# The lead-in of a four-layer transformer tower: one pass over all tokens against one pass per group of tokens

## The reference

```python
h = layer_norm(emb_word[input_ids] + emb_pos[:S][None], emb_ln_s, emb_ln_b)
for l in range(4):
    q = heads(h @ Wq[l] + bq[l]); k = heads(h @ Wk[l] + bk[l]); v = heads(h @ Wv[l] + bv[l])
    a = band_attention(q, k, v, mask)            # each token sees 64 tokens to each side
    h = layer_norm(h + a @ Wo[l] + bo[l], ln1_s[l], ln1_b[l])
    h = layer_norm(h + gelu(h @ W1[l] + b1[l]) @ W2[l] + b2[l], ln2_s[l], ln2_b[l])
```

## Time and profile before

| | |
|---|---|
| time, median of 3 runs | 1876.82 us (1876.59 to 1877.55) |
| span of the profiled execution (first to last instruction) | 1874.5 us, that is 2.3 us less than the median |
| PE busy | 1483.1 us (79% of the span) |
| DVE busy | 1247.8 us (67%) |
| ACT busy | 977.2 us (52%) |
| POOL busy | 808.0 us (43%) |
| mean granted TensorE clock | 0.895 of full speed |

### The profile page before, as it was taken

How to read it: one execution, slowest core, us unless ns; L and a number is a source line. 1 busy time by engine, 2 the same in 40 slices (tenths; PEclk the granted TensorE clock), 3 DMA queues, 4 the chain that set the end, 5 groups by cost and what they waited for, 6 DMA issues and landing times.

```text
span 1874.5 us, 42615 instructions
## 1 busy us (share of the span) xinstructions
PE 1483.1 (79%) x13098; PEld 1235.0 (66%) x13098; DVE 1247.8 (67%) x3542; ACT 977.2 (52%) x2392; POOL 808.0 (43%) x1177
## 2 busy tenths in 40 slices
PE   0589889798897997998988759759668887499992
PEld 0367678677676776776767648449646766389992
DVE  4788966788767888668896652433379896434344
ACT  0378733688434885348873223225348882155550
POOL 6577333684235762247733310124356521144440
PEclk9899989899899997999998968669869996599996
DMA  4666101743005550035610000147534511257765
GB/s 105 176 149 127 36 1 33 170 86 84 1 5 138 108 121 2 1 70 140 128 33 1 1 14 1 45 138 224 173 89 100 112 22 45 97 175 237 225 212 179
DMA packets 144317, 178.26 MB, mean 95 GB/s; under 512 B 22096, under 2 KB 106128, under 8 KB 143952
## 3 DMA queue, kind: packets, MB, share of 16 engines
q1 hardware_dynamic: 136784, 158.18, 32.9%
q0 software_dynamic: 7296, 17.18, 2.8%
HBM read 132.96 MB, written 42.34 MB: 94 GB/s over the span
## 4 chain that ended last, share of the span: by engine, by line
PE 31%; DVE 14%; issue 4%; DMA 2%; ACT 2%; POOL 2%; SPq 0%; DVEq 0%; POOLq 0%; ACTq 0%
PE bank L1473 7%; DVE ptl L799 4%; PE bank L1459 2%; DVE neg_max L792 2%; PE bank L645 1%; DVE xn L912 1%; PE bank L563 1%; PE bank L1460 1%; PE bank L1463 1%; PE bank L1461 1%; PE bank L1462 1%; PE bank L1217 1%; DMA xn<-y_rows 1%; PE bank L431 1%; PE bank L584 1%
## 5 line engine op out<-in xcount | busy, mean ns | idle before, releaser
L685 ACT ACTIVATE prob<-bank,neg_max 128x192 f32<-128x192 f32 (+1 forms) x960 | 406.9, 437 | 109.3 <-DVE neg_max L792 97.0
L792 DVE TENSOR_REDUCE neg_max<-bank 128x2 f32<-128x384 f32 (+1 forms) x480 | 274.3, 572 | 99.0 <-PE bank L544 91.4
L799 DVE TENSOR_TENSOR ptl<-bank,pth 128x384 f16<-128x384 f32 (+1 forms) x480 | 275.5, 574 | 4.6 <-ACT pth L698 4.0
L563 PE MATMUL bank<-ident,prob 128*128 128x128 f32 x1536 | 268.4, 288 | 0.0
L698 ACT ACTIVATE pth<-bank 128x384 f16<-128x384 f32 (+1 forms) x480 | 244.3, 509 | 9.3 <-PE bank L563 9.2
L652 ACT ACTIVATE xx<-bank 128x256 fp32r<-128x256 f32 x256 | 95.5, 386 | 196.0 <-PE bank L431 192.0
L544 PE MATMUL bank<-kx,qx 96*128 96x192 bf16 (+1 forms) x960 | 168.1, 257 | 1.1 <-DVE xx L766 1.1
L563 PEld LDWEIGHTS bank<-ident,prob 128*128 128x128 f32 x1536 | 162.9, 143 | 0.1
L584 PE MATMUL bank<-v,pth 128*128 128x33 bf16 x1152 | 138.4, 180 | 21.2 <-DVE ptl L799 18.0
L645 PE MATMUL bank<-w,fbuf 128*128 128x192 f32 x768 | 140.7, 327 | 2.0 <-DVE h L889 2.0
L734 ACT ACTIVATE fbuf<-bank,b 128x512 f32<-128x512 f32 x96 | 65.8, 687 | 146.5 <-PE bank L453 146.4
(11 more groups left out here) (295 smaller groups left out, 4522.5 us busy)
## 6 DMA issues: line engine op xcount, KB each, us to landing
xn<-in_e_seg SPq DMA_DIRECT2D x34, 768.0 KB
w<-in_e_w SPq DMA_DIRECT2D x23, 576.0 KB
qk_rows<-fbuf SPq DMA_DIRECT2D x128, 96.0 KB, 2.3
qx<-qk_rows SPq DMA_DIRECT2D x35, 288.0 KB, 4.0
kx<-qk_rows SPq DMA_DIRECT2D x35, 288.0 KB, 5.8
qk_rows<-w SPq DMA_DIRECT2D x80, 96.0 KB, 2.3
qx<-qk_rows SPq DMA_DIRECT2D x35, 192.0 KB, 4.6
kx<-qk_rows SPq DMA_DIRECT2D x35, 192.0 KB, 5.2
```

What stands on the lines that cost most here:

```text
L563: last = nc.tensor.transpose(bank[BT[p % 2]][:, c * P:c * P + P], probs_at(p, banded, c * P, P), ident[:, :])
L685: nc.scalar.activation(probs_at(p, banded, qt * n, n), scores_at(p, n)[:, qt, :], ACT.Exp, bias=neg_max[:, b % 2, hd, qt:qt + 1], scale=1. ...
L792: nc.vector.tensor_reduce(neg_max[:, b % 2, hd, :], scores_at(p, D if banded else S), AX.X, ALU.max, negate=True).then_inc(max_ready.sem, 1)
L799: nc.vector.tensor_tensor(ptl[:, p % 2, 0:n], bank[BT[p % 2]][:, 0:n], pth[:, p % 3, 0:n], ALU.subtract)\
```

## The change

- **Position rows.** They are loaded into `places`, a part of `prob` that the attention does not yet use, and after the token numbers instead of ahead of them.
- **Gathers.** Each group has a semaphore of its own. POOL issues 8 gathers, then does the `rstd` of group 0 (for which it waits), then issues the other 8.
- **Weights.** ACT makes the two high parts as its first work, DVE the scaled bias and the two low parts. POOL has no part in it.
- **Norms by group.** DVE adds the position rows of group 0 in one instruction, does its statistics, builds the first half of `mask` while POOL makes `rstd`, does scale and shift, and builds the second half of `mask`. Then it goes through `OPENING`, with the sums and statistics of group 1 after the first 4 tiles, those of group 2 and scale and shift of group 1 after v, and those of group 3 and scale and shift of group 2 at the end.
- **POOL.** The `rstd` of groups 2 and 3 and the `hb` sums of groups 1 and 2 come after `pool_v`.
- **Table fills.** The 8 DMAs that fill `y_rows`, with the wait for `mask_ok`, are issued after the last layer's SP work.

```diff
@@ sync
-            sp.dma_start(hb[:, 0:2, :], a["L0_tok_emb_pos"]).then_inc(const_in.sem, 16)
             sp.dma_start(tok[:, :], a["x"]).then_inc(tok_in.sem, 16)
+            sp.dma_start(places, a["L0_tok_emb_pos"]).then_inc(const_in.sem, 16)
...
             load_x(0)
             sp.dma_start(row_bo[:, :], a["bo"][0, :, :].to_broadcast([P, D])).then_inc(rows_bo.sem, 16)
-            sp.wait_ge(mask_ok.sem, 1)
-            filler = flat(mask[:, :, :], "p t d -> p (t d)").bitcast(F32).rearrange("p (t d) -> p t d", d=D)
-            for s in range(2):
-                for i in range(4):
-                    sp.dma_start(y_rows[s][8 * P * i:8 * P * (i + 1), :].rearrange("(t p) d -> p t d", p=P), filler)\
-                        .then_inc(filled.sem, 16)
...
             sp_layer(L - 1)
             sp.wait_ge(wa_ready.sem, wa_ready.at(L, 1))
+            sp.wait_ge(mask_ok.sem, 1)
+            (the same 8 DMAs)
 
             sp.wait_ge(h_ready.sem, h_ready.at(L, 0))
@@ gpsimd
-                    .then_inc(gathered.sem, 16)
-            pool.wait_ge(rows_x.sem, 48)
-            pool.wait_ge(const_in.sem, 16 * 8)
-            ch.mark(nc.gpsimd.tensor_tensor(bqk[:, :], bqk[:, :], q_scale[:, :].to_broadcast([P, 3]), ALU.mult))
-            pool_weights(ch, wa, QKV).then_inc(wa_ready.sem, 1)
+                    .then_inc(gathered[t // GT].sem, 16)
+                if t == 2 * GT - 1:
+                    pool_rstd(pool, ch, 0, 1 - NG, 0, 1e-12)
+            pool_rstd(pool, ch, 0, 2 - NG, 1, 1e-12)
+            pool_ones(ch)
             pool.wait_ge(rows_bo.sem, 16)
-            for g in range(NG + 1):
-                if g < NG:
-                    pool_rstd(pool, ch, 0, g + 1 - NG, g, 1e-12)
...
+            first_sums(0)
...
             pool_v(pool, ch, 0, 0)
+            pool_rstd(pool, ch, 0, 3 - NG, 2, 1e-12)
+            for g in range(NG):
+                pool.wait_ge(gathered[g].sem, 16 * GT)
             pool_middle(pool, ch, 0, 0)
             pool_middle(pool, ch, 0, 1)
+            pool_rstd(pool, ch, 0, 4 - NG, 3, 1e-12)
+            first_sums(1)
+            first_sums(2)
@@ scalar
+            act.wait_ge(rows_x.sem, 48)
+            nc.scalar.activation(wa[0][:, 0:QKV], raw[:, 0, 0:QKV], ACT.Copy)
+            nc.scalar.activation(wa[2][:, 0:QKV], raw[:, 1, 0:QKV], ACT.Copy).then_inc(first_high.sem, 1)
             for kind, i in OPENING:
@@ vector
-            dve.wait_ge(gathered.sem, 16 * NT)
-            for t in range(NT):
-                ch.mark(nc.vector.tensor_tensor(h[:, t, 0:D], h[:, t, 0:D], hb[:, t % 2, :], ALU.add))
...
+            dve.wait_ge(rows_x.sem, 48)
+            dve.wait_ge(first_high.sem, 1)
+            (bqk, wa[1] and wa[3]: three tensor_tensor)
+            dve.sem_inc(wa_ready.sem, 1)
...
+            def first_norm(g):
+                tg = slice(GT * g, GT * g + GT)
+                rows = h[:, tg, 0:D].rearrange("p (b t) d -> p b t d", t=2)
+                dve.wait_ge(gathered[g].sem, 16 * GT)
+                ch.link(nc.vector.tensor_tensor(rows, rows, places.unsqueeze(1).to_broadcast([P, 2, 2, D]), ALU.add))
+                dve_stats(dve, ch, 0, 0, g, None)
...
+            first_norm(0)
+            first_mask(range(2 * GT))
+            first_affine(0)
+            first_mask(range(2 * GT, NT))
+            ch.done(ch.n)
+            dve.sem_inc(mask_ok.sem, 1)
+            first_open(OPENING[0:GT])
+            first_norm(1)
+            first_open(OPENING[GT:2 * GT + 3])
+            first_norm(2)
+            first_affine(1)
+            first_open(OPENING[2 * GT + 3:])
+            first_norm(3)
+            first_affine(2)
```

More of the change, by code:

```diff
@@ L209, in build_tower @@
                   for x in (probs[:, PROBS * 2 * D:PROBS * 2 * D + HEADS * VC], sb("middle", [P, HEADS * VC])[:, :])]
+        places = probs[:, 0:2 * D].rearrange("p (t d) -> p t d", t=2)
         prob_16 = flat(prob[:, :, :, :], "p a s n -> p (a s n)").bitcast(BF16)
@@ L257, in build_tower @@
         tok_in = sig("tok_in", base=0)
-        gathered = sig("gathered", base=0)
+        gathered = [sig(f"gathered_{g}", base=0) for g in range(NG)]
+        first_high = sig("first_weights_high", base=0)
         tok_ok = sig("tok_ok", base=0)
@@ L1682, in _ @@
             sp.wait_ge(wa_ready.sem, wa_ready.at(L, 1))
+            sp.wait_ge(mask_ok.sem, 1)
+            filler = flat(mask[:, :, :], "p t d -> p (t d)").bitcast(F32).rearrange("p (t d) -> p t d", d=D)
+            for s in range(2):
+                for i in range(4):
+                    sp.dma_start(y_rows[s][8 * P * i:8 * P * (i + 1), :].rearrange("(t p) d -> p t d", p=P), filler)\
+                        .then_inc(filled.sem, 16)
             sp.wait_ge(h_ready.sem, h_ready.at(L, 0))
@@ L1942, in _ @@
-            ch.done(ch.n)
[L1943 to L1948, removed]
-                        dve.sem_inc(h_ready.sem, (12, 4)[g - 1])
-                    dve_affine(dve, ch, 0, g - NG, g - 1, 1)
+            dve.wait_ge(rows_x.sem, 48)
+            dve.wait_ge(first_high.sem, 1)
+            ch.mark(nc.vector.tensor_tensor(bqk[:, :], bqk[:, :], q_scale[:, :].to_broadcast([P, 3]), ALU.mult))
@@ new lines, in _, with first_mask @@
+            ch.mark(nc.vector.tensor_tensor(wa[1][:, 0:QKV], raw[:, 0, 0:QKV], wa[0][:, 0:QKV].bitcast(F32), ALU.subtract))
+            ch.mark(nc.vector.tensor_tensor(wa[3][0:D2, 0:QKV], raw[0:D2, 1, 0:QKV], wa[2][0:D2, 0:QKV].bitcast(F32),
+                                            ALU.subtract))
+            ch.done(ch.n)
+            dve.sem_inc(wa_ready.sem, 1)
+            def first_mask(tiles):
+                for t in tiles:
+                    qt = t % 2
+                    ch.mark(nc.vector.tensor_tensor(mask[:, t, :], hb[:, 4 + qt, :],
+                                                    km[:, t // 2, qt * WIN:qt * WIN + D], ALU.min))
@@ new lines, in first_norm, with first_affine @@
+            def first_norm(g):
[4 more added lines that the diff above has]
+                dve_stats(dve, ch, 0, 0, g, None)
+            def first_affine(g):
+                if g < 2:
+                    dve.sem_inc(h_ready.sem, (12, 4)[g])
+                dve_affine(dve, ch, 0, g + 1 - NG, g, 1)
@@ L1957, in dve_layer, with first_open @@
                          if opening else None)
-            for kind, i in OPENING:
-                dve_open(dve, ch, 0, kind, i, True, first_split(0))
+            def first_open(items):
+                for kind, i in items:
+                    dve_open(dve, ch, 0, kind, i, True, first_split(0))
+            first_norm(0)
[12 more added lines that the diff above has]
+            first_affine(2)
             with dve.Fori(0, L - 1) as it:
```

11 lines of the change are left out of this document (4 added, 7 removed).

## The result

| | before | changed |
|---|---|---|
| median | 1876.59 us (5 runs, 1870.13 to 1877.55) | 1856.33 us (5 runs, 1850.11 to 1864.33) |
| span of the profiled execution | 1874.5 us | 1854.6 us |
| mean granted TensorE clock | 0.895 | 0.892 |

The ratio is 0.9912, with a 95% interval of 0.9889 to 0.9936. That is 12 to 21 us less; the forecast was 1856.6. The changed kernel's five runs lie 14 us apart, and their clocks (0.885 in the slowest, 0.895 in the fastest) go with their times. So single medians say little about an effect of a few us here.

A forecast was written before the change was run, and what follows sets the result against it. DVE was taken to set the pace, idle 17.43 us in the lead-in for the sixteenth gather. First maximum 19.0 earlier plus 1.2 gave 20.2: 1874.5 - 20.2 = 1854.3, with 2.3 around it 1856.6 us; range 1851 to 1863.

The forecast's parts named there:

- Steps 1 to 4: Lead-in: token numbers, weights, norm and rstd of group 0; DVE free at about 19.5, rstd ready at 25.8 us.
- Step 5: Scale and shift of group 0 on DVE: 3.9 us, done at 29.7, PE starting at about 28.
- step 6: Second half of the mask (2.2 us), then splits of group 0 (2.47): last split starts at 34.35, 29.8 earlier.
- step 7: DVE from group 0's last split to the end of v: still 12.39 us, group 1's norm fitting into a wait.
- Step 8: Work new on DVE between v and the first maximum: 15.9 us, first maximum at 62.65, 19.0 earlier.
- Step 9: Start of the attention: PE's work done ahead shortens DVE's waits between first maxima by 1.2 us (bounds 0 and 3.9).
- The stretched gathers: Rival: gathers 5 to 8 lengthen beside DVE's work, group 0's rstd is 7.5 us late, time 1864; chance 0.15.
- Nothing is carried: Rival: layer 0's attention waits for something that has not moved, time stays near 1876 us; chance 0.02.
- The sign of being wrong: The prediction would be wrong if the distance from the first maximum to the first MLP had grown.
- Costed at nothing: Moving the table fills, and moving the weights off POOL by itself, were each taken to gain nothing.
- the prediction's rule: Gathers beside additions, statistics and the rest of the mask keep 0.95 us each, since tensor_tensor does not lock GpSimd out.

The follow-up runs named there:

- Sums_later: The changed kernel with POOL's four sums of group 0 behind the rstd of group 3 instead of ahead of v; median 1854.20 us, ratio 0.9888 to the kernel before.
- All_gathered: The changed kernel with DVE waiting for all 16 gathers before each norm, first rstd behind all gathers; median 1871.88 us, ratio 0.9986 to the kernel before.
- ramp_warm: The changed kernel with 20 extra unread transposes on PE ahead of the second chunk of group 1 in each layer; 1861.73 us in one run.
- fills_late_only: The kernel before with only the 8 table fills moved behind the last layer; median 1879.02 us, ratio 1.0028 to the kernel before.
- short_affine: The changed kernel without scale and shift of group 2, one copy in their place; 1853.59 us in one run.
- mask_and_sums: The changed kernel with group 0's sums later and the mask's second half behind group 0's splits; median 1850.87 us, ratio 0.9875 to the kernel before.
- pool_weights: The changed kernel with the weights split on POOL again, behind its 16 gathers; median 1862.24 us, ratio 0.9937 to the kernel before.
- fills_again: The kernel before with only the 8 table fills moved behind the last layer, run a second time; ratio 0.9997 to the kernel before.

## Why the prediction was right, point by point

The forecast of the whole lay 0.3 us off, and this is better than its parts deserve: errors of up to 2.8 us cancelled, and the scatter of the runs is larger than 0.3 by itself. That they cancelled is luck; that the lead of the first maximum reaches the end is not. The changed kernel is ahead by 19.3 us at the first maximum (forecast 19.0), 20.5 at "wb", 21.7 at "MLP", and 21.2 at SP's first issue after the layers (1077.06, now 1055.84), and its span is 19.9 shorter (forecast 20.2).

- **Steps 1 to 4** gave 2.5 us more than forecast: group 0 was added at 18.27 (19.5), DVE had its `rstd` at 23.26 (25.8). The gather of the first tile began at 8.85 instead of 9.98, for the token numbers landed 1.1 sooner, not 0.5. And the fifth gather took 1.52, not 3.46. DVE waited 0.41 for `rstd` where I had 1.4.
- **Step 5** was 0.5 too long (3.4 measured), step 6 right to 0.2: the last split came 32.6 earlier, forecast 29.8. PE's first transpose came at 25.45 instead of some 28.
- **Steps 7 and 9 are those whose reasoning failed,** by 2.4 us each. In step 7 I let the stretch to the end of v stand at 12.39. It took 14.8, since POOL's sums of group 0 now run beside DVE's pieces. Sums_later shows it: without them it is 12.39. The Trainium skill, "SBUF — State Buffer", section "Who interferes with whom", has the rule: a VectorE instruction with two SBUF inputs, or in a two-port mode, and a GpSimd instruction that reads SBUF block each other. The rows agree: the four forms take 0.86, 0.96, 1.07 and 0.70 beside POOL's additions, 0.43, 0.69, 0.68 and 0.43 without. I had weighed the rule for the gathers only. That DVE and POOL "meet only at semaphores and at DMAs", as I wrote at the top, is not the whole of it. The four instructions make 1.4 of the 2.4 us; the rest is DVE's waiting for v, 1.21 and 0.71 instead of 0.63 and 0.34 in sums_later.
- **Step 8** was right: 16.0 from the end of v to the first maximum, forecast 15.9, at 62.37 instead of 62.65. All_gathered shows that order alone is worth 0.9 to 1.6 up to there.
- **Step 9 had the wrong sign.** PE's lead was to give 1.2 back; the stretch grew by 1.2 instead. PE's second chunk of group 1, before and changed:

```profile
85.04 0.79 PE L449 MATMUL bank<-xx,wa_hi 128*128 128x512 f32 x1
```

```profile
65.78 0.80 PE L451 MATMUL bank<-xx,wa_hi 128*128 128x512 f32 x1 [5.38 <-ACT qf L672]
```

  It begins 3.41 us behind the first maximum in both (3.39 to 3.41 in all ten kernels of the table). PE did its first scores and first chunk ahead, as forecast, but the second waits for ACT's copy of the first, which stands in ACT's queue behind its table load and the first exponentials, and these need the first maximum. So the lead could buy nothing: I had the path wrong. From the start of this chunk to the first low part it takes 3.75 before, at a granted clock of 0.87, and 4.95 in the changed kernel at 0.50, which is the 1.2. It takes 3.34 in ramp_warm and 3.33 in fills_late_only, both at 1.00. So the clock is the cause, and short_affine shows that a shorter gap alone doesn't cure it.
- **What made up for it** was not foreseen. From first low part to "wb" the changed kernel takes 33.5, the one before 36.0. In the old one POOL's pieces of group 1 ran beside DVE's scale and shift of group 3. The rows of that line from the trace, before and changed:

```profile
L848 DVE SCALAR_TENSOR_TENSOR hb<-h,mv,ln_s x4: 403/1229/1349, 91.8 to 105.8; 128x192 f32<-128x192 f32 x4
```

```profile
L850 DVE SCALAR_TENSOR_TENSOR hb<-h,mv,ln_s x4: 405/478/1075, 74.3 to 85.9; 128x192 f32<-128x192 f32 x4
```

  The rows give minimum/median/maximum in ns: a median of 478 instead of 1229. All 12 instructions of this scale and shift took 9.18 us in the stretch before and 6.54 in the changed kernel, and DVE's whole busy time fell from 33.66 (78 instructions) to 30.86 (79). Its idle time did not fall (2.31 and 2.66), so PE's higher clock in this stretch (0.98 against 0.91) does not explain the 2.5 us. No run took POOL's pieces away from beside DVE's, so this rests on the traces.
- **The rivals.** The stretched gathers did not come ahead of `rstd` of group 0: gathers 5 to 8 took 1.52, 0.95, 0.94, 0.95. The second eight had one of 3.42, and POOL still finished them at 36.1, ahead of need; `rstd` of group 2 was ready at 56.5 (forecast 56.6), DVE wanted it at 58.1. "Nothing is carried" is refuted by the marks of the whole change above, and by short_affine and mask_and_sums: 3.8 us at the first maximum are 3.7 and 4.2 at "wb". The sign of being wrong that hangs on it did not come: from the first maximum to "MLP" it takes 159.7 us, before 162.2.
- **Costed at nothing.** The fills' move was rightly costed in both orders; SP now issues them from 932.28 to 948.43 and has nothing more to issue until 1055.84. The weights' move was not: pool_weights prices it at 7.5 us in the new order. The sum was right in spite of this, as it counted the weights as done in time.

## What to carry to other kernels

When many transfers feed a chain and only the first few are needed to start it, give each group a semaphore; but look for everything else that stands behind the last transfer on the issuing engine, for the gain is that of the later of the two (here 14.8 us at the first maximum with the weights moved, 7.5 less without). Work pushed out of the path comes back further on: count it up to the next mark at which an engine is saturated, not to where it left. Place small additions on POOL into stretches where DVE waits, since here each slowed the other's (POOL's four additions took 3.31 us beside DVE's pieces, and in sums_later twelve took 6.64). Before you count on an engine's lead, ask whose output its next piece of work waits for, and look at the granted clock behind the wait that the lead creates.

## What was not expected of the hardware

- A gather's issue beside DVE's work takes 0.94 to 1.04 us in most cases, and up to 3.46 in some. In all 13 traces, each of the 46 gathers that took more than 1.25 us ends 0.12 or 0.82 us (within 0.02) after the end of an instruction of DVE, or of a run of them; of the 78 that took less than 1.00 and began before 30 us only 2 do. The large `tensor_scalar` and cast instructions show both distances (in the changed kernel 11.54 + 2.41 = 13.95, DVE's end at 13.83; 14.25 + 1.66 = 15.91, DVE's end at 15.10).
- Behind `tensor_tensor` it is 0.82, so the prediction's rule that these leave the gathers alone does not hold here. The gather of 3.42 in the changed kernel ends at 29.74 and the second half of the mask at 28.91; the 3.46 of the kernel before ends at 20.84 and the mask at 20.02. The addition of group 0 does it as well, in pool_weights:

```profile
17.89 0.96 DVE L1954 TENSOR_TENSOR h<-h,prob 128x768 f32<-128x768 f32 x1 [2.62 <-DMA h<-in_L_tok_emb_word,au]
18.20 1.47 POOL L1738 DMA_INDIRECT h<-in_L_tok_emb_word,au  x1 [0.30 <-issue]
```

  It ends at 19.67, the addition at 18.85. One gather of 3.42 to 3.46 occurs in seven of the ten kernels traced first, always with a run of small mask instructions. Why most gathers beside the same instructions slip through, no run shows. In the new order it cost nothing.
- In the old order the gather of 3.46 is on the path to the first maximum. The last gather ends at 34.60 with it, and at 32.53 and 32.78 in fills_late_only and fills_again, where no gather took so long; the first addition follows 2.7 to 2.8 us later in all three (37.44, 35.22, 35.59). So some 2 us of the lead at the first maximum hang on which trace of the old order it is measured against. Whether the long gather belongs to the kernel before or to that one execution is open, for it was traced once.
